# Taking the second-layer accumulator of a feed-forward chunk out of PSUM bank by bank

## The reference

```
x = x + 0.5 * ffn0(layernorm(x));  x = x + attn0(layernorm(x));  x = x + 0.5 * ffn0(layernorm(x))
x = x + 0.5 * ffn1(layernorm(x));  x = x + attn1(layernorm(x));  x = x + 0.5 * ffn1(layernorm(x))

ffn0(x) = gelu(x @ proj1.T + b1) @ proj2.T + b2                 # 256 -> 1024 -> 256
ffn1:  six times  x = gelu(x @ W1.T + B1) @ W2.T + B2 + x,      # and layernorm(x) * G + B after each but the last
```

## Time and profile before

| | |
|---|---|
| three runs | 2843.85, 2886.33, 2926.83 us |
| median | 2886.33 us |
| profiled execution | 2873.61 us, its span 2871.8 us |
| mean granted TensorE clock | 0.943 of full speed |
| busy share of the span | PE 90%, PEld 75%, DVE 65%, ACT 48%, POOL 19% |

### The profile page before, as it was taken

How to read it: one execution, slowest core, us unless ns; L and a number is a source line. 1 busy time by engine, 2 the same in 40 slices (tenths; PEclk the granted TensorE clock), 3 DMA queues, 4 the chain that set the end, 5 groups by cost and what they waited for, 6 DMA issues and landing times. The chain is left out here.

```text
span 2871.8 us, 50876 instructions
## 1 busy us (share of the span) xinstructions
PE 2590.3 (90%) x17384; PEld 2145.0 (75%) x17384; DVE 1875.8 (65%) x3906; ACT 1368.5 (48%) x2422; POOL 547.5 (19%) x365
## 2 busy tenths in 40 slices
PE   4985999959899999996899999999999599999998
PEld 3863545438788888886778878878878588888888
DVE  4566756455667776765567767667677667767763
ACT  3421545544444444453455555555555344444453
POOL 1000000030324433411111001001000423424420
PEclk9985858879999999998999999999999799999999
DMA  3034313010000000000000000000000100000000
GB/s 149 0 89 125 44 26 46 3 59 1 30 0 30 30 0 29 0 1 18 19 19 1 19 19 0 19 19 0 19 29 2 59 0 30 1 29 29 0 0 29
DMA packets 18980, 73.70 MB, mean 26 GB/s; under 512 B 3328, under 2 KB 8192, under 8 KB 15616
## 3 DMA queue, kind: packets, MB, share of 16 engines
q1 hardware_dynamic: 18816, 71.78, 8.7%
HBM read 61.02 MB, written 10.49 MB: 25 GB/s over the span
## 5 line engine op out<-in xcount | busy, mean ns | idle before, releaser
L315 PEld LDWEIGHTS ps<-w,hid 128*128 128x128 f32 x5376 | 699.1, 191 | 94.6 <-issue 56.8
L315 PE MATMUL ps<-w,hid 128*128 128x256 f32 x5376 | 719.2, 284 | 35.1 <-DVE rb L377 32.2
L290 PE MATMUL ps<-xT,w 128*128 (+1 forms) x2688 | 706.5, 399 | 0.0
L451 DVE TENSOR_TENSOR hid<-gel,hid 128x512 fp32r<-128x512 f32 x448 | 439.1, 991 | 392.7 <-ACT hid L354 384.2
L348 ACT ACTIVATE gel<-ps,b 128x512 f32<-128x512 f32 x448 | 307.3, 687 | 643.1 <-issue 624.0
L290 PEld LDWEIGHTS ps<-xT,w 128*128 128x128 f32 x2688 | 481.6, 191 | 79.2
L354 ACT ACTIVATE hid<-gel 128x512 fp32r<-128x512 f32 x448 | 272.7, 621 | 0.0
L731 PE MATMUL ps<-pT,v_sb 128*128 128x512 f32 (+3 forms) x1152 | 261.4, 357 | 3.0 <-DVE pT L834 3.0
L704 PE MATMUL ps<-k_sb,q_sb 128*128 128x512 f32 (+3 forms) x1152 | 252.0, 352 | 5.8 <-DVE q_sb L851 5.7
L1273 DVE TENSOR_REDUCE nmx<-ps 128x1 f32<-128x512 f32 (+3 forms) x384 | 196.0, 553 | 83.7 <-PE ps L1140 50.3
L823 DVE TENSOR_REDUCE negmax<-ps 128x1 f32<-128x128 f32 (+7 forms) x256 | 192.0, 752 | 72.7 <-PE ps L707 71.7
(11 more groups left out here) (111 smaller groups left out, 3204.8 us busy)
## 6 DMA issues: line engine op xcount, KB each, us to landing
wraw<-in_wffn SPq DMA_DIRECT2D x11, 2048.0 KB, 7.6
xb<-in_w_a SPq DMA_DIRECT2D x8, 1280.0 KB, 5.6
qk_dram<-rope_hl SPq DMA_DIRECT2D x16, 512.0 KB, 3.0
xT<-qk_dram SPq DMA_DIRECT2D x60, 128.0 KB, 8.2
xb<-in_wffn SPq DMA_DIRECT2D x3, 2048.0 KB, 12.6
qk_own<-qk_dram SPq DMA_DIRECT2D x36, 128.0 KB, 6.6
x<-in_x SPq DMA_DIRECT2D x4, 512.0 KB, 5.5
rot<-in_rot SPq DMA_DIRECT2D x1, 2048.0 KB, 18.7
```

Of the source, the lines that this page charges most:

```text
L290: last = nc.tensor.matmul(ps[:, HPS + j % 4, :], w[par][:, wp, 0, k * HIDDEN + j * PART:k * HIDDEN + (j + 1) * PART], xT[:, xp, k, bass.ds ...
L315: last = nc.tensor.matmul(y_ps[:, t, :], hid[:, hp, j % 4, t * PART:(t + 1) * PART], w[par][:, wp, 1, j * DIM:(j + 1) * DIM], start=j == 0 ...
L451: nc.vector.tensor_tensor(hid[:, 1, j % 4, :], gel[:, j % 4, :], hid[:, 0, j % 4, :].bitcast(f32), ALU.subtract).then_inc(low_done, 1)
```

## The change

- VectorE takes the accumulator with two instructions of 512 columns, bank 4 (token tiles 0 and 1) first, then bank 5. Each counts up `y_free`, which so goes to 2 per chunk.
- A new semaphore, `y_half`, is counted by TensorE with the last matmul of token tile 1 in the last `pe_second` of a chunk: bank 4 is complete there, six matmuls ahead of bank 5. The first VectorE instruction waits for `y_half`, the second for `mm2_done` as before.
- In the first `pe_second` of a chunk TensorE waits for `y_free` twice: ahead of token tile 0 for bank 4, ahead of token tile 2 for bank 5. Both waits now stand behind the wait for `low_done`.
- VectorE's own wait, for what reads `rb` next, goes to the second count.

```diff
         def pe_second(pe, at, j):
             g, s, c, blk, par, kind = at
-            if j == 0:
-                wait(pe, y_free, g)
             pe.wait_ge(low_done, HT * g + j + 1)
             for t in range(TPC):
+                if j == 0 and t % 2 == 0:
+                    wait(pe, y_free, 2 * g - 1 + t // 2)
                 for n, (hp, wp) in enumerate(PARTS):
                     last = nc.tensor.matmul(
...
+                if j == HT - 1 and t == 1:
+                    last.then_inc(y_half, 1)
             last.then_inc(mm2_done, 1)
...
         def dve_take(dve, p, at):
-            dve.wait_ge(mm2_done, HT * g + HT)
             if p.l1:
                 dve.wait_ge(xb_ready, p.xb0 + CHUNKS * blk + c + 1)
-                add = xb[:, tiles, :]
-            else:
-                add = rows[:, B2_0:B2_0 + 1, :].broadcast_to([PART, TPC, DIM])
-            nc.vector.tensor_tensor(rb[:], y_ps[:, :, :], add, ALU.add).then_inc(y_free, 1)
-            dve.wait_ge(y_free, g + 1)
+            for bank in range(2):
+                two = slice(2 * bank, 2 * bank + 2)
+                if p.l1:
+                    add = xb[:, bass.ds(c * TPC + 2 * bank, 2), :]
+                else:
+                    add = rows[:, B2_0:B2_0 + 1, :].broadcast_to([PART, 2, DIM])
+                if bank == 0:
+                    dve.wait_ge(y_half, g + 1)
+                else:
+                    dve.wait_ge(mm2_done, HT * g + HT)
+                nc.vector.tensor_tensor(rb[:, two, :], y_ps[:, two, :], add, ALU.add).then_inc(y_free, 1)
+            dve.wait_ge(y_free, 2 * g + 2)
```

More of the change, by code:

```diff
@@ L151, in build @@
         mm2_done = sem("mm2_done")
+        y_half = sem("y_half")
         y_free = sem("y_free")
```

## The result

Over 22 executions each the changed kernel takes 2840.87 us in the median (2814.03 to 2907.56), the kernel before 2864.86 us (2843.85 to 2926.83), a ratio of 0.992. That ratio is 0.990, with a 95% interval of 0.987 to 0.992: 22 to 37 us. In a later session it was 0.989 (0.984 to 0.993). That lies within 2%, and clear of no change.

A forecast was written before the change was run, and what follows sets the result against it. TensorE was taken to bound the FFN, stopped by the take. Gains of 23.8 (44 ordinary chunks), 0 (8 splitting chunks) and 1.1 us (tails) sum to 24.9 of 2873.61 us: 2848.7 profiled, 2861 as median, range 2822 to 2902.

The forecast's parts named there:

- the ordinary chunks: The 44 FFN chunks without weight splitting, where TensorE stops for the take: 0.54 us gained each, 23.8 us together.
- the tails: The four phase ends: 0.54 us gained at the program's end, 0.2 us in each of three others, together 1.1 us.
- who is late at the take: VectorE's queue reaches the take behind low(1), after both banks are complete, so `y_half` brings nothing in the loop.
- (1): Take in two on VectorE: second instruction starts 0.60 us behind the first; VectorE 0.06 us longer, which is hidden.
- (2): TensorE's first wait: bank 4 free 0.54 us sooner, gain 0.54 us per ordinary chunk, 0.18 us of the stop stays.
- (3): TensorE's wait for bank 5 at token tile 2: met with 0.15 us cover, cost nothing; bounds 0 and 0.25 us.
- The 8 chunks: Chunks with weight splitting: the 0.54 us gained at the take is waited out for `xn`; gain 0, bounds -0.06 and +0.54.
- A: Rival: TensorE's stop at the take vanishes whole, 39.6 us gained, 2847 us; chance 0.08.
- B: Rival: transposes wait for `xn` in ordinary chunks too, gain given back, only tails left, 2885 us; chance 0.12.
- C: Rival: second take instruction held up, TensorE stops again at bank 5's wait, 57 us slower, 2943 us; chance 0.03.
- D: Rival: 25 us more of FFN work at the 1.2 GHz clock level cancels the gain, 2886 us; chance 0.04.

The follow-up runs named there:

- the single release: Changed kernel, but TensorE waits ahead of token tile 0 for both banks at once; ratio to the kernel before 1.001 (0.997 to 1.004).
- the early take: Changed kernel with the take moved from behind low(1) to behind low(0) on VectorE; to the kernel before 0.987 and 0.988, without `y_half` 0.992 and 0.993.

## Why the prediction was right

**Forecast and size.** It was 24.9 us of 2873.61, a ratio of 0.9913; measured are 0.990 and 0.989, and the forecast lies in both intervals. The forecast of the median, 2861 us, is 20 us above the measured 2840.87, nearly all of it because the kernel before has 2864.86 us over 22 executions and not the 2886.33 us of the first three. By the FFN phases alone the change gave 21.7 us. That 24.9 comes so near is in part luck: the ordinary chunks gave 3 us more than forecast, and falls of the clock, which the sum didn't have, took 4 to 7 us. With 6 us for them it is 26.8 + 0.9 - 6 = 21.7 us; the 0.9 are the tails.

**What bounds, and who is late at the take.** Right. The take starts 0.67 us after mm1(3), as before, and `y_half` is without effect in the loop (shown by its removal).

**(1) and (2), the first half.** The mechanism was right (shown by the single release, which gives everything back) and the size a little low: 0.61 us instead of 0.54. The missing 0.07 us is mostly the way from the end of the VectorE instruction to the weight load. I took 0.12 us from the single take; behind the halves it is 2305.07 - (2304.33 + 0.68) = 0.06 us. The weight load so starts at T + 1.41 instead of T + 1.46, and the next mm1 follows it after 1.53 us instead of 1.55. The recorded 1.22 us of the long instruction is thus not the whole time to its release, and in this case the difference of the two durations undersized what the shorter one gives. 44 x 0.61 = 26.8 us instead of 23.8.

**(3), the second wait.** Right: no stop. Its cover was put at 0.15 us. In the changed kernel it is T + 1.41 + 0.75 less the release at T + 1.95 + 0.06, again 0.15 us, and the instruction between the halves gives some 0.17.

**The 8 chunks.** Right in mechanism: what the stop at the take gives (0.61 us) the wait for `xn` takes. By the steps of a block, 100.3 - 98.5 = 1.8 = 3 x 0.61, nothing stays. The wait itself grew to 2.2 us and not to the 2.3 of the forecast, as 0.17 us of the gain show just ahead of it. What I did not have is the clock's fall behind this wait, below.

**The tails.** 0.53 us at the end, forecast 0.54. Of the three others, put at 0.2 us each, two gave 0.17 us (the transposes behind the phase wait 8.19 instead of 8.36 us for `xn`) and the first gave nothing (9.67 us in both). Together 0.9 instead of 1.1 us.

**Rivals.** A (the stop gone whole) did not happen, as 0.11 us stay; it takes the early take to get there. B (gain given back in ordinary chunks) did not: the waits for `xn` are still 17. C needs a late second half; with one made 0.33 us late the kernel was still faster than before, as it should be up to 0.69. D (clock) happened in a small way and at a place that I had not named: not in the dense stretches but behind the waits of the transposes. Three falls of 1.4 to 1.8 us each in the first profile of the changed kernel, and four in the second, take 4 to 7 us of the 27.

## What to carry to other kernels

When an accumulator is handed back late, look first at what the releasing engine does before it gets to it. Here an earlier signal was worth nothing in the loop, because another instruction stood ahead in the queue, while releasing the first bank by itself took 0.61 us of a stop of 0.72. The second half needs no earlier release than the reader's own way to it, and a half more in the queue cost no time there. Check the segments where another engine sets the pace: what the first stop gives, the next wait takes, and the clock may fall behind a longer wait. And when a gain is as small as the spread between executions, sum the phases that the change touches: here they agreed within 0.2 us between two profiles whose totals lay 38 us apart.

## What the runs showed of the hardware

**The clock behind a wait of 2.2 us.** In the eight chunks with weight splitting TensorE waits for `xn`: 1.76 to 2.03 us in the kernel before and 1.8 us in the one with a single release, 2.2 us in the nine profiles with a bank-wise release or the early take (one wait of 2.47). In the 20 us behind such a wait the mean granted clock was 1.00 in 15 of 16 cases with the shorter wait, and 0.91 in one. With the longer one it was 0.91 or 0.92 in 34 of 72 cases and 1.00 in the others. TensorE had done nothing but wait for these 2.2 us, and worked all but without a break behind them. In some cases the transposes right behind the wait already show it, with up to 1.97 us instead of 1.09, the time of 8 of them at the lower of the two levels of 2.4 and 1.2 GHz; in others the fall comes a little later. With GpSimd's work cut, and these waits gone, the granted clock of the two kernels was 1.00 over both stretches of 400 us that I looked at:

```profile
840.00:1240.00 400.00, 397.83 (x2544) 356.61 (x2544) 283.41 (x587) 202.17 (x319) 132.10 (x82) 1.00 0.04 16
```

So with the change a rare fall of the clock became one in nearly every second case. That the 0.43 us more of idle are the cause is not shown. The longer wait never came alone: with it the stops at the takes were shorter. And among the waits of 2.2 us the counts lean with these stops: the clock fell in 5 of 16 cases in the two kernels whose step from mm1(3) is 3.0 to 3.4 us, in 10 of 24 where it is 2.94, and in 19 of 32 where it is 2.83. No run lengthens this wait and leaves the stops as they were. Why the fall comes behind one and not the other wait of the same length stays open too.

**A wait met on an idle VectorE.** In the kernel with the whole take behind low(0), VectorE is idle when the matmul that the take waits for ends. In the timeline above it started 0.25 us after that end (2344.99 to 2345.24), and within 0.05 us at the end of the program. Over the 52 takes of that kernel's loop it is 0.04 us in eight and 0.13 to 0.34 us in 44. All six takes of the first two phases, which add the bias row (`rows`) and have no wait for `xb_ready`, are among the eight, those inside the loop over chunks included; the other two take `xb` like the 44. So neither the idle queue nor the loop alone makes the difference, and what does was not tried. In the changed kernel, where an earlier instruction still runs when the sum ends, none of this was seen.
